# One expert layer of a mixture-of-experts block in split single-pass products, and its other weights fetched per tile

## The reference

```python
gate_weights = jax.nn.softmax(x @ gate_w + gate_b, axis=-1)
topk_vals, topk_idx = jax.lax.top_k(gate_weights, TOP_K)          # TOP_K = 2 of NE = 8
h = gelu(einsum('bse,neh->bsnh', x, w1) + b1)                     # 128 -> 256
h = gelu(einsum('bsnh,nhk->bsnk', h, w2) + b2)                    # 256 -> 256
expert_out = einsum('bsnh,nhe->bsne', h, w3) + b3                 # 256 -> 128
return sum(topk_vals * expert_out[topk_idx])
```

## Time and profile before

| what | value |
|---|---|
| runs before | 621.4, 620.99, 623.19 us; median 621.4 |
| the profiled execution's own time | 621.06 us, of which its span 619.5 us |
| busy share of the span | PE 95%, ACT 86%, DVE 59%, POOL 34% |
| chain that ended last | PE 60%, DVE 17%, ACT 13% |
| first layer 1 (tile -2) to first late score | 292.9 to 418.83 us |
| granted TensorE clock, mean | 0.998 |

### The profile page before, as it was taken

One profiled execution on the slowest core, in us unless ns is written; L12 is line 12 of the kernel. 1 busy time (PEld: TensorE's weight loads), 2 busy tenths in 40 slices (PEclk: granted clock), 3 DMA queues, 4 the chain that ended last, 5 costly groups with the idle time before them and its releaser, 6 DMA issues.

```text
span 619.5 us, 12074 instructions
## 1 busy us (share of the span) xinstructions
PE 588.0 (95%) x4106; PEld 252.2 (41%) x4106; DVE 365.2 (59%) x805; ACT 531.5 (86%) x541; POOL 211.6 (34%) x188
## 2 busy tenths in 40 slices
PE   7889999999999998999999999999999999999996
PEld 5323332222222222222899999993222222222221
DVE  5754224856462432121555555655778889898866
ACT  3699999999999999999455455559999999999995
POOL 2700000000554545442122222123867658686100
PEclk9999999999999999999999999999999999999999
DMA  8564601641464546492533333310212121221311
GB/s 234 159 217 168 241 34 52 222 171 52 154 221 162 176 139 205 146 302 54 123 74 78 74 75 77 75 44 18 78 66 90 43 78 60 64 76 64 115 47 38
DMA packets 83294, 70.68 MB, mean 114 GB/s; under 512 B 45344, under 2 KB 59072, under 8 KB 83248
## 3 DMA queue, kind: packets, MB, share of 16 engines
q1 hardware_dynamic: 76528, 56.47, 30.1%
q0 software_dynamic: 5856, 13.05, 6.7%
q10 hardware_dynamic: 864, 0.58, 0.4%
HBM read 32.92 MB, written 32.96 MB: 106 GB/s over the span
## 4 chain that ended last, share of the span: by engine, by line
PE 60%; DVE 17%; ACT 13%; issue 8%; DMA 1%; POOL 1%; ACTq 0%; SPq 0%; POOLq 0%; DVEq 0%
PE ps L1639 13%; PE ps L1573 10%; PE ps L1623 8%; DVE probs L1323 7%; ACT probs L745 7%; PE ps L1586 5%; PE ps L1565 5%; PE ps L1703 5%; ACT probs L780 4%; PE ps L1535 4%; PE ps L1671 3%; ACT probs L723 2%; DVE probs L1325 2%; DVE x_all L1266 2%; PE ps L1480 2%
## 5 line engine op out<-in xcount | busy, mean ns | idle before, releaser
L745 ACT ACTIVATE probs<-ps 128x1536 f32<-128x1536 f32 (+1 forms) x154 | 204.9, 1439 | 3.2 <-PE ps L1623 3.0
L780 ACT ACTIVATE probs<-ps 128x1536 f32<-128x1536 f32 x140 | 189.8, 1511 | 1.7 <-PE ps L1671 1.5
L621 POOL DMA_INDIRECT slots_x_d<-xn_all,slot_i x64 | 63.2, 988 | 191.5 <-PE ps L1639 181.1
L659 POOL DMA_INDIRECT work<-slots_y_d,slot_i x64 | 105.8, 1653 | 47.5 <-PE ps L1703 30.7
L1639 PE MATMUL ps<-probs,v_st 128*32 128x512 f32 x896 | 119.3, 605 | 0.6 <-ACT probs L745 0.6
L759 ACT ACTIVATE work<-ps,work 128x256 f32<-128x256 f32 (+1 forms) x156 | 64.9, 455 | 60.4 <-PE ps L1573 60.2
L1703 PE MATMUL ps<-probs,v_st 128*32 128x512 f32 x840 | 111.5, 604 | 0.0
L1623 PE MATMUL ps<-q_st,k_st 32*128 32x512 f32 x448 | 76.3, 494 | 5.9 <-ACT probs L745 5.7
L1671 PE MATMUL ps<-q_st,k_st 32*128 32x512 f32 x420 | 71.1, 494 | 7.7 <-ACT probs L780 7.2
L1623 PEld LDWEIGHTS ps<-q_st,k_st 32*128 32x128 f32 x448 | 28.9, 181 | 117.5 <-ACT probs L745 102.4
L1671 PEld LDWEIGHTS ps<-q_st,k_st 32*128 32x128 f32 x420 | 26.5, 181 | 106.8 <-ACT probs L780 98.8
(11 more groups left out here) (206 smaller groups left out, 541.3 us busy)
## 6 DMA issues: line engine op xcount, KB each, us to landing
k_d<-parts SPq DMA_DIRECT2D x8, 1024.0 KB, 5.2
q_d<-parts SPq DMA_DIRECT2D x8, 1024.0 KB, 6.1
q_st<-q_d SPq DMA_DIRECT2D x30, 256.0 KB, 3.6
k_st<-k_d SPq DMA_DIRECT2D x30, 256.0 KB, 2.7
slots_x_d<-parts SPq DMA_DIRECT2D x5, 1024.0 KB, 7.9
work<-slots_x_d SPq DMA_DIRECT2D x128, 32.0 KB, 1.9
slots_y_d<-work POOLq DMA_DIRECT2D x32, 128.0 KB, 2.2
work<-work SPq DMA_DIRECT2D x24, 128.0 KB, 2.0
```

The source lines that it names most:

```text
L659: nc.gpsimd.indirect_dma_start(out=gath[:, i % 2, GATHER * c + k, :], out_offset=None, in_=slots_y_d, in_offset=bass.IndirectOffsetOnAxis( ...
L745: nc.scalar.activation(group_probs(phase, g)[:, 0:size, :], group_slot(g)[:, 0:size * HALF].rearrange("p (h n) -> p h n", n=HALF), ACT.Exp ...
L780: nc.scalar.activation(late_probs(g), group_slot(g).rearrange("p (h n) -> p h n", n=HALF), ACT.Exp, scale=SCALE).then_inc(S["exp_done"], 1)
```

## The change

Layer 2 of pair tiles (all but tile -2) is no longer one float32 product but three fp32r products whose sum stands for it: weights and hidden numbers are split into a high part (rounded to fp32r) and a low part (the rest), and high x high, high x low and low x high are added in PSUM. So four products of a tile become twelve. The high part of the weights is made by DVE (a copy that rounds, from `w_all`), their low part by POOL (a subtraction), the high part of the hidden numbers by ACT (a copy that rounds), their low part by DVE (a subtraction). These parts lie in a new tensor `split`, which shares its place with `xn_all`; every writer first waits until all rows are scattered.

`w_all` now holds only layer 2, so step 7 has 8 weight transfers in place of 24. Layers 1 and 3 come for each tile straight from the inputs: SP reads the tile's expert number into a register and issues one transfer for layer 1 and one for layer 3, each of 128 KB, into the same two staging buffers. DVE's copies of them are gone, and so is the copy of the bias of layer 3. The bias of layers 1 and 2 has four buffers, and its copy is an addition of zeros now. DVE, POOL and SP are written out tile by tile, without a loop; PE and ACT keep theirs. Layer 1 and its gelu run one tile further ahead.

```diff
+LAST_TILE = SLOT_TILES - 3
+def split_tile(n):
+    return n % 6 != 5 and n != -2
...
+        xn_at = -(-nc.sbuf_base // 32) * 32
         xn_all = sb("xn_all", [P, TILES, C])
+        split = nc.alloc_sbuf_tensor_at("split", [P, 4, 2, 2 * HID], F32R, offset=xn_at)
...
             def load_expert(e):
-                sp.dma_start(w_all[:, e, 0:HID], w1[e]).then_inc(S["w_loaded"], 16)
                 sp.dma_start(w_all[:, e, HID:3 * HID]...
-                sp.dma_start(w_all[:, e, 3 * HID:WCOLS]...
+            def load_w1(n, e):
+                j = slot_tile(*tile_of(n))[0]
+                if n >= 0:
+                    sp.wait_ge(S["l1_done"], j * 2 - 2)
+                sp.dma_start(w1_sb[:, n % 2], w1[bass.ds(e, 1)].rearrange("a p n -> p (a n)")).then_inc(w1_loaded[n % 2], 16)
+            def load_w3(n, e):
+                if n >= 0:
+                    sp.wait_ge(S["l3_done"], slot_tile(*tile_of(n))[0] - 1)
+                sp.dma_start(w3_sb[:, n % 2], w3[bass.ds(e, 1)].rearrange("a (k p) n -> p (a k) n", p=P)).then_inc(w3_loaded[n % 2], 16)
+            def which_expert(n):
+                return sp.value_load(expert_i[0:1, bass.ds(slot_tile(*tile_of(n))[3], 1)], min_val=0, max_val=E_ - 1)
...
-                        for n in range(-2, 2):
+                        load_rows(0, -2, True)
+                        expert = which_expert(-2)
+                        load_w1(-2, expert)
+                        load_w3(-2, expert)
+                        load_rows(0, -1, True)
+                        expert = which_expert(-1)
+                        load_w1(-1, expert)
+                        load_w3(-1, expert)
+                        for n in range(2):
                             load_rows(0, n, True)
...
-            for n in range(2, CYCLE):
-                load_rows(0, n)
-            with sp.Fori(1, CYCLES) as i:
-                for n in range(CYCLE):
-                    load_rows(i, n)
-            load_rows(CYCLES, 0)
+            expert = which_expert(0)
+            for n in range(LAST_TILE + 2):
+                if n <= LAST_TILE:
+                    load_w1(n, expert)
+                if n + 2 <= LAST_TILE:
+                    load_rows(*tile_of(n + 2))
+                if n >= 1:
+                    load_w3(n - 1, before_expert)
+                if n < LAST_TILE:
+                    before_expert, expert = expert, which_expert(n + 1)
+                else:
+                    before_expert = expert
...
+            def lower_w2(i, n, e):
+                if split_tile(n):
+                    pool.wait_ge(S["w2_made"], slot_tile(i, n)[0] + 1)
+                    nc.gpsimd.tensor_tensor(w2_low[:, n % 2], w_all[:, bass.ds(e, 1), HID:3 * HID].rearrange("p a n -> p (a n)"),
+                                            w2_high[:, n % 2].bitcast(F32), ALU.subtract).then_inc(S["w2_low_made"], 1)
...
+            def gelus(i, n):
+                gelu(i, n + 1, 0)
+                high_hidden(i, n + 1)
+                gelu(i, n, 1)
...
+            for n in range(LAST_TILE + 3):
+                if 1 <= n <= LAST_TILE + 1:
+                    stage_w2(*tile_of(n - 1), made[n - 1])
+                if n <= LAST_TILE:
+                    turn_rows(*tile_of(n))
+                    stage_b12(n, made[n])
+                if n >= 1:
+                    finish_y(*tile_of(n - 3), made[n - 3], n < 3)
+                if 1 <= n <= LAST_TILE + 1:
+                    low_hidden(*tile_of(n - 1))
+                if n < LAST_TILE:
+                    made[n + 1] = expert_of(slot_tile(*tile_of(n + 1))[3])
...
+                        if split_tile(n):
+                            for term, (w, h) in enumerate(((w2_high, h1_high), (w2_high, h1_low), (w2_low, h1_high))):
+                                ins = nc.tensor.matmul(h2_ps[m][:, 0:2 * ST], w[:, par, lo:lo + P], h[:, par, k * HID:k * HID + 2 * ST],
+                                                       start=(k == 0 and term == 0), stop=(k == 1 and term == 2))
...
                 for n in range(CYCLE):
-                    layer1(i, n)
-                    if n >= 1:
-                        layer3(i, n - 1)
-                    else:
-                        layer3(i - 1, CYCLE - 1)
+                    layer1(i, n + 1)
+                    layer3(i, n - 1)
                     layer2(i, n)
```

More of the change, by code:

```diff
@@ L319, in build @@
         w2_sb = w_st[:, :, HID:3 * HID].rearrange("p a (k n) -> p a k n", k=2)
+        w2_high, w2_low, h1_high, h1_low = (split[:, k] for k in range(4))
         w3_sb = w_st[:, :, 3 * HID:WCOLS].rearrange("p a (k n) -> p a k n", k=2)
@@ L641, in store_y @@
                                y_sb[:, n % 2, 0:units]).then_inc(y_stored[n % 2], 16)
[L643 to L648, removed]
+            e = pool_expert(0, 0)
+            for n in range(LAST_TILE + 1):
+                if n >= 1:
+                    store_y(*tile_of(n - 3))
+                lower_w2(*tile_of(n), e)
+                if n < LAST_TILE:
+                    e = pool_expert(*tile_of(n + 1))
+            for n in range(LAST_TILE - 2, LAST_TILE + 1):
+                store_y(*tile_of(n))
             pool.wait_ge(y_stored[0], 16 * ((SLOT_TILES + 1) // 2))
@@ L751, in _, with gelu, high_hidden @@
                 group_exps(t, t % 2)
[L753 to L760, removed]
+            def gelu(i, n, layer):
+                j, units = slot_tile(i, n)[0:2]
+                rows, par = slice(0, units * ST), n % 2
+                ready, signal, src, dst = (("l1_done", "g1_done", h1_ps, h1), ("l2_done", "g2_done", h2_ps, h2))[layer]
+                if layer == 0:
+                    act.wait_ge(S["b12_made"], j + 1)
+                for k in range(2):
+                    act.wait_ge(S[ready], j * 2 + (k + 1))
+                    nc.scalar.activation(dst[:, par, k, rows], src[k][:, rows], ACT.Gelu, bias=b12_st[:, n % 4, layer, k:k + 1])\
+                        .then_inc(S[signal], 1)
+            def high_hidden(i, n):
+                if split_tile(n):
+                    act.wait_ge(S["g1_done"], slot_tile(i, n)[0] * 2 + 2)
+                    nc.scalar.activation(h1_high[:, n % 2], h1_all[:, n % 2], ACT.Copy).then_inc(S["h1_high_made"], 1)
+            def gelus(i, n):
+                gelu(i, n + 1, 0)
+                high_hidden(i, n + 1)
+                gelu(i, n, 1)
+            gelu(0, -2, 0)
+            act.wait_ge(S["x_scattered"], 16 * 2 * TILES)
             gelus(0, -2)
@@ L766, in _ @@
                     gelus(i, n)
-            gelus(CYCLES, 0)
+            gelu(CYCLES, 0, 1)
             nc.scalar.activation(fb[:, 3:4], zeros[:, 0:1], ACT.Exp)
@@ L1232, in _ @@
             normalise(SPLIT - 1)
[L1234 to L1244, removed]
-                else:
[L1246 to L1256, removed]
+            dve.wait_ge(S["x_scattered"], 16 * 2 * TILES)
+            for n in range(LAST_TILE + 3):
[4 more added lines that the diff above has]
+                    stage_b12(n, made[n])
+                if n >= 1:
+                    finish_y(*tile_of(n - 3), made[n - 3], n < 3)
+                if 1 <= n <= LAST_TILE + 1:
+                    low_hidden(*tile_of(n - 1))
+                if n < LAST_TILE:
+                    made[n + 1] = expert_of(slot_tile(*tile_of(n + 1))[3])
+            finish_y(*tile_of(LAST_TILE), made[LAST_TILE])
             def combine(i):
```

97 lines of the change are left out of this document (56 added, 41 removed).

## The result

The changed kernel takes 645.0 us (median; 644.6 to 645.98), beside 621.2 for the kernel before (a fourth run added to the three shown above), 23.8 more: ratio 1.038, 95% interval 1.036 to 1.040. The profiled execution, the longest of the four, took 645.98 us (span 644.1), 24.9 more than that of before.

A forecast was written before the change was run, and what follows sets the result against it. SP's queue was to bound the kernel at 3.60 us per tile against PE's 3.20: tile 36 13.3 us late plus 1.4 of longer end chain, 14.7 us on 621.06, gives 635.8 us, range 622 to 648.

The forecast's parts named there:

- SP as the bound: SP's six issues and a register read per tile exceed PE's 3.20 us by 0.40 us; chance 0.76.
- SP's turn: SP's queue, per tile: 0.38 to first row, 1.92 to layer 3, 1.30 with layer 3's issue and read; 3.60 us.
- The start: Before tile 0: 23 issues and three reads put its layer 1 issue at 299.8, landing at 301.8.
- landing: Layer 1's weight transfer was to land 2.0 us after its issue; tile 36's at 429.0.
- tail: Chain from tile 36's layer 1 to the late scores: 4.6 us instead of 3.14, 1.4 more.
- PE, layer 2: Twelve fp32r products with hidden loads take 1.34 us in place of 1.73; PE's pair tile falls to 3.09 us.
- that rival: Layer 2's weight loads on PE don't hide: 2.6 us for layer 2, 651 us in all; chance 0.08.
- PE stays the bound: Rival: SP's issues overlap its reads, PE sets the pace at 2.87 us per tile, 612 us; chance 0.07.
- DVE and POOL: Rival: the two engines block each other, 3.15 us per tile, 622 us, no change; chance 0.09.
- The lock: DVE's small bias addition waits while POOL subtracts (1.36 us), as the two exclude each other.
- What costs nothing: Weight issues gone from step 7, DVE, ACT and POOL work below 3.60 us, and waits over before SP reaches them.

The follow-up runs named there:

- the run that made it true: Changed kernel with no weights fetched per tile: all in `w_all`, DVE copies layer 1's, PE reads layer 3's in place; 614.8 us, ratio 0.9888 to the kernel before.

## Why the prediction was right, and where its size was off

The forecast was 635.8 us in a range of 622 to 648, with SP as the bound. The mechanism is shown: the waits name it, a read less takes the loss away, an issue more adds to it, and the rivals' edits change nothing. The size was 14.7 us forecast, 24.9 measured between the profiled executions (23.8 between the medians), so terms of the sum were too small: the mean turn of SP, the start of the stage and the last tile.

**SP's turn.** Forecast 3.60 us for each of 34 turns. The typical turn shown above is 3.62, made of 0.41, 2.03 and 1.18 where I had 0.38, 1.92 and 1.30. But the mean is larger. Issues of layer 1 for tile 2, tile 35 and tile 36:

```profile
309.26 0.37 SPq L463 DMA_DIRECT2D work<-in_L_ffn_w_dram  x1
...
432.91 0.37 SPq L463 DMA_DIRECT2D work<-in_L_ffn_w_dram  x1
...
434.62 0.34 SPq L463 DMA_DIRECT2D work<-in_L_ffn_w_dram  x1
```

(432.91 - 309.26) / 33 = 3.75, so 33 x 0.15 = 4.9 us more than forecast. Medians hid this: some reads take 0.54 rather than 0.27, and single row issues take over a microsecond. The two turns with such an issue (from 323.94 and 343.17) last 4.40 and 4.76 and make up 2.0 of the 4.9. In the second, at 343.58, three issues last 2.21 instead of about 1.4:

```profile
343.58 2.21 SPq L481 DMA_DIRECT2D work<-slots_x_d  x3
```

The forecast's sum came close to the typical turn by errors that cancel: layer 3's issue with the read was shorter (1.18 against 1.30; the load alone 0.27 against 0.305), the other issues stood further apart (0.41 and 2.03 against 0.38 and 1.92). The Trainium skill's floor of some 600 ns for such a load (DMA: Bandwidth & Descriptors, Latency and other measured facts) does not agree with this trace, 0.27 in the median; the measurement decides.

**The start.** Forecast: layer 1 of tile 0 issued at 299.8, of tile 1 at 302.9, of tile 2 at 302.9 + 3.6 = 306.5. They came at 301.22, 304.30 and 309.26, so 1.4, 1.4 and 2.8 late. About 1.2 is the longest of the row issues, 1.67 us instead of 0.45, ahead of tile 0's. Another 1.2 is a wait that I had called over: in tile 1's turn SP stood at the fetch of tile 0's layer 3 until PE had done layer 3 of tile -2, which has the same buffer (the row from 306.14 ends at 308.06; SP issued at 308.08). SP's waits from 304 to 309 us, and PE there:

```profile
SPq L469 <- PE ps L1668: 1.2, 1, 1.2
```

```profile
304.30 2.05 PE L1636 MATMUL ps<-work 128*128 128x256 f32 x4 [5.53 <-DMA work<-in_L_ffn_w_dram]
...
306.14 1.92 PE L1668 MATMUL ps<-work 128*128 128x128 f32 x8
307.84 1.71 PE L1656 MATMUL ps<-work 128*128 128x128 f32 x8
309.39 1.03 PE L1636 MATMUL ps<-work 128*128 128x256 f32 x4
```

```profile
304.00:309.00 5.00, 4.70 (x18) 4.38 (x19) 0.79 (x2) 1.63 (x4) 0.07 (x1) 0.50 0.33 62
```

PE was idle for 5.53 us, and after it ran at a granted clock of 0.50, the 1.2 GHz level: layer 1 took 2.05 us instead of 1.03. The forecast had layer 1 of tile 0 at 301.8. It began at 304.30, since its transfer was issued 1.4 late and PE started only 3.1 after the issue, where I had put 2.0 for landing; that PE is slow behind such idle time was not in the forecast at all.

**Landing, and the last tile.** From tile 2 on 33 turns lead to tile 35's issue at 432.91, 7.6 after the forecast's 425.3, and tile 36's at 434.62 (427.0). By the 2.2 us of landing (2.0 in the earlier trace rows) it was there at 436.8. But PE was still at layer 2 of tile 34 then and began tile 36 at 438.26, 9.3 after the forecast's 429.0. The tail, on PE:

```profile
438.26 1.02 PE L1636 MATMUL ps<-work 128*128 128x256 f32 x4
439.12 1.05 PE L1668 MATMUL ps<-work 128*128 128x128 f32 x8
440.01 1.06 PE L1656 MATMUL ps<-work 128*128 128x128 f32 x8
441.17 0.84 PE L1668 MATMUL ps<-work 128*128 128x128 f32 x4
441.77 1.68 PE L1653 MATMUL ps<-split 128*128 128x256 f32 x12
443.38 0.50 PE L1753 MATMUL ps<-q_st,k_st 32*128 32x512 f32 x3
```

5.1 us, where 4.6 was forecast: I had followed ACT and DVE, but PE's own order puts layers 2 and 3 of older tiles ahead of tile 36's layer 2. Together 443.38 - 418.83 = 24.6 us: the forecast's 14.7, 2.8 at the start, 4.9 of turns, 1.7 at tile 36 and 0.5 of tail.

**PE, layer 2.** Forecast 1.34 us for twelve products, 0.111 apart; the run without the read shows 1.43 (370.28 to 371.70 in its chain, and 3.18 - 0.86 - 0.89), 0.12 apart. The loads hide, so that rival falls. As SP was the bound, the difference cost nothing here. For the rival "PE stays the bound" (612 forecast) it matters: a cycle of 18.11 us and 614.8 us in the run that made it true.

**DVE and POOL.** The lock was forecast as it came: the addition takes 0.88 us beside POOL, 0.12 without it. The Trainium skill's rule of exclusion (SBUF — State Buffer, Who interferes with whom) agrees; that it also bars a plain copy of weights (1.35 against 0.28) is in the trace as well. As the bound this rival falls by three runs: without the split, with the addition ahead, and with both the read and the lock gone.

**What costs nothing.** That the waits in SP's queue are over when SP gets there held from tile 2 to tile 36's layer 1, not in tile 1's turn.

## What to carry to other kernels

Count every instruction of the issuing queue for one turn of the loop, register reads included, and hold the sum against the time per turn of the engine that sets the pace: 3.6 against 3.2 us decided this change, while no busy share showed it. For the size, take the mean with its outliers rather than the median, since nothing in a queue that is full makes up for a long one. Work that is spared on the bounding engine (7 us of PE here) pays only if what feeds it gets no slower; an SBUF copy on an engine with room did better than a fetch through a full queue.

## What the runs showed that was not expected

- After idle times of 5.53 us (changed kernel), 4.25 us (tile 0's fetch earlier) and 3.83 us (without the read, with the addition ahead) PE ran layer 1 in 2.05, 2.07 and 2.04 us; after 3.10 us of idle time (without the read) it took 1.10, at a granted clock of 1.00.
- Of 156 row issues on SP with a median of 0.45 us, three took 1.2 to 1.7 us. They don't look like chance: with the addition ahead, with tile 0's fetch earlier and with one issue less, row issues of over a microsecond stand at the same three places, one among the rows of tiles 0 and 1 and one in each of the turns of tiles 6 and 11. Without the split there are two (turns of tiles 6 and 12), with one issue more none. What holds them up is open.
- A read of a register on SP took 0.27 us at most times and up to 0.54 at others, on DVE 0.30 to 0.56, on POOL 0.28 to 0.71.
